# Two transfers for the transposition of x, largest scores ahead of rotated queries in two steps of four, and a high half behind the next exponents

## The reference

```python
x = x + xattn(layernorm(x), ctx, ctx, Wq, Wk, Wv, Wo)
x = x + ffn(layernorm(x), w_gate, w_up, w_down)

# xattn: q, k, v = h @ Wq, ctx @ Wk, ctx @ Wv, split in 16 heads; rotary embedding on q and k
score = einsum('bhqd,bhkd->bhqk', qh, kh) / sqrt(32)
out = einsum('bhqk,bhkd->bhqd', softmax(score), vh)      # then merged heads @ Wo

# ffn: act_qdq rounds to 16 bits by the tensor's largest magnitude; weights to 4 bits in blocks of 32
h = act_qdq(h)
up, gate = act_qdq(h @ qdq(w_up).T), act_qdq(h @ qdq(w_gate).T)
gate = act_qdq(gate * fixed_qdq_u16(sigmoid(gate)))
out = act_qdq(gate * up) @ qdq(w_down).T
```

## Time and profile before

| | us |
|---|---|
| median of 3 runs | 2328.13 (2327.36 to 2330.8) |
| the profiled execution | 2326.45 |
| its span, first to last instruction | 2324.6 |
| PE busy | 2203.7 (95%) |
| DVE busy | 1685.1 (72%) |
| ACT busy | 1329.8 (57%) |
| POOL busy | 701.5 (30%) |
| PE busy, 200 to 300 / 300 to 400 / 500 to 600 us | 87.3 / 93.1 / 93.7 |

### The profile page before, as it was taken

One profiled execution on the slowest core, in us unless ns is written; L12 is line 12 of the kernel. 1 busy time (PEld: TensorE's weight loads), 2 busy tenths in 40 slices (PEclk: granted clock), 3 DMA queues, 4 the chain that ended last, 5 costly groups with the idle time before them and its releaser, 6 DMA issues. The chain is left out here.

```text
span 2324.6 us, 31131 instructions
## 1 busy us (share of the span) xinstructions
PE 2203.7 (95%) x12037; PEld 971.1 (42%) x12037; DVE 1685.1 (72%) x1690; ACT 1329.8 (57%) x1299; POOL 701.5 (30%) x655
## 2 busy tenths in 40 slices
PE   5898999999998899999999999999998799999999
PEld 3443333333333444444444444444443344444444
DVE  7656788889876766445543598888888887778773
ACT  3345566666654233222322787877877777777772
POOL 3444566666664301000100264444444000000000
PEclk8899999999999999999999999999999899999999
DMA  6333667777777577888875898877776555655552
GB/s 189 97 103 101 168 173 189 170 193 173 193 169 182 154 232 244 265 245 254 255 229 180 286 336 306 303 283 290 292 281 260 188 223 221 235 220 204 209 217 91
DMA packets 286711, 500.14 MB, mean 215 GB/s; under 512 B 187500, under 2 KB 189804, under 8 KB 249692
## 3 DMA queue, kind: packets, MB, share of 16 engines
q1 hardware_dynamic: 286556, 498.09, 66.9%
HBM read 247.75 MB, written 186.58 MB: 187 GB/s over the span
## 5 line engine op out<-in xcount | busy, mean ns | idle before, releaser
L1694 PE MATMUL banks<-XB,W 128*128 128x512 f16 x2304 | 498.9, 380 | 2.3 <-ACT XB L1720 2.3
L1694 PE MATMUL banks<-XB,WT 128*128 128x512 f16 x2304 | 497.4, 379 | 0.0
L2160 PE MATMUL banks<-W,OH 128*128 128x512 f16 x2256 | 488.8, 380 | 2.5 <-DVE OH L2262 2.5
L1714 ACT ACTIVATE OB<-banks,uns 128x512 f32<-128x512 f32 x384 | 255.7, 684 | 391.2 <-PE banks L1694 388.6
L1694 PEld LDWEIGHTS banks<-XB,W 128*128 128x128 f16 x2304 | 225.7, 98 | 275.1 <-issue 3.4
L1694 PEld LDWEIGHTS banks<-XB,WT 128*128 128x128 f16 x2304 | 225.4, 98 | 271.8
L2160 PEld LDWEIGHTS banks<-W,OH 128*128 128x128 f16 x2256 | 221.1, 98 | 270.2 <-DVE OH L2262 3.0
L1981 POOL TENSOR_TENSOR PR<-GS,OB 128x2048 f32<-128x2048 f32 x46 | 220.6, 4795 | 257.5 <-ACT OB L1714 247.6
L1803 DVE TENSOR_REDUCE amx<-OB 128x1 f32<-128x2048 f32 x48 | 109.7, 2285 | 238.2 <-ACT OB L1714 238.2
L748 PE MATMUL banks<-XC,AH 128*128 128x512 f16 x768 | 179.3, 385 | 3.2 <-POOL AH L1506 1.6
L689 PE MATMUL banks<-XD,WQ 128*128 128x512 f16 x768 | 179.2, 383 | 2.5 <-DVE WQ L1127 1.2
(11 more groups left out here) (272 smaller groups left out, 2904.5 us busy)
## 6 DMA issues: line engine op xcount, KB each, us to landing
g_s<-OB SPq DMA_DIRECT2D x48, 1024.0 KB, 6.1
GL<-g_s SPq DMA_DIRECT2D x48, 1024.0 KB, 7.5
up_s<-OB SPq DMA_DIRECT2D x48, 1024.0 KB, 4.9
XA<-up_s SPq DMA_DIRECT2D x32, 1024.0 KB, 9.3
gq_s<-GQ SPq DMA_DIRECT2D x48, 512.0 KB, 4.8
XD<-gq_s SPq DMA_DIRECT2D x48, 512.0 KB, 6.7
XA<-in_x SPq DMA_DIRECT2D x16, 1024.0 KB, 6.7
QW<-QE SPq DMA_DIRECT2D x128, 128.0 KB, 2.9
```

The lines of the kernel that those rows point to most:

```text
L1694: t = e.matmul(pk[:].rearrange("p (j t) -> p j t", j=4), WT[w][:, ot, wa, kk, :], XB[i % 2][:, xa, :, kk, :], start=(kk == 0 and wa == 0 a ...
L1714: e.activation(OB[n % 3][:, r, :], bank[(k + 4) % 8][:], ACT.Copy, scale=uns[:, 12 * w + ot:12 * w + ot + 1]).then_inc(s_ev, 1)
L2160: t = e.matmul(pk[:].rearrange("p (r n) -> p r n", r=4), OH[i % 2][:, a, ot, j * 128:(j + 1) * 128], WD[:, :, c, wa, o4, :], start=(ot == ...
```

## The change

Three edits, all in the attention. `sp_x_turn` gets a half `a`, waits for the high parts (a = 0) or the low parts (a = 1) alone and transposes 16 blocks; up to step 15 both halves stand where the one transfer stood, later the first half stands in c = 1 at the old place and the second in c = 2, behind the swap and ahead of the load of x. All counts of `s_xt` double. `dve_largest` is the old maxima block as a function, and in steps 16 to 65 with c = 0 or c = 3 it is called ahead of the rotary addition. `act_a_high` is the old high half as a function; from step 16 on, the second unit's is called in the next step behind the exponents.

```diff
-            e.wait_ge(s_xlo, 2 * b + 2)
+            e.wait_ge((s_xhi, s_xlo)[a], 2 * b + 2)
...
-            e.dma_start_transpose(XD[b % 2][:].rearrange("p a j (k t) -> p (a j k) t", t=128),
-                                  ST.rearrange("p a j d -> p (a j d)")).then_inc(s_xt, 16)
+            e.dma_start_transpose(XD[b % 2][:, a, :, :].rearrange("p j (k t) -> p (j k) t", t=128),
+                                  ST[:, a, :, :].rearrange("p j d -> p (j d)")).then_inc(s_xt, 16)
...
                 for nb in [1] if s == 2 else x_at(s, 2):
-                    sp_x_turn(e, nb)
+                    sp_x_turn(e, nb, 0)
+                    if s < 16:
+                        sp_x_turn(e, nb, 1)
+                for nb in x_at(s - 1, 2) if s > 16 else []:
+                    sp_x_turn(e, nb, 1)
                 if c == 2 and 2 <= b + 2 < B:
                     sp_x_load(e, b + 2)
...
                     e.activation(P[0:SK], PB[0:SK, 0:4, :], ACT.Exp, scale=SM_SCALE).then_inc(s_p, 1)
+                for u in normal_at(s - 1)[1:] if s > 16 else []:
+                    act_a_high(e, u)
...
-                for u in normal_at(s):
...
+                for u in normal_at(s)[:1] if 16 <= s < NSTEP - 1 else normal_at(s):
+                    act_a_high(e, u)
...
+                largest_first = 16 <= s < NU + 2 and c in (0, 3)
+                if largest_first:
+                    dve_largest(e, s - 2)
                 if 1 <= s <= NU:
                     dve_rope_add(e, ROT["q", s - 1])
...
-                if 0 <= u < NU:
...
+                if 0 <= u < NU and not largest_first:
+                    dve_largest(e, u)
```

More of the change, by code:

```diff
@@ L424, in sp_x_load, with sp_x_turn @@
             e.dma_start(X[:], x1_rows(b)).then_inc(s_x, 16)
-        def sp_x_turn(e, b):
-            e.wait_ge(s_xlo, 2 * b + 2)
+        def sp_x_turn(e, b, a):
+            e.wait_ge((s_xhi, s_xlo)[a], 2 * b + 2)
             if b == 1:
@@ L561, in sp_attention @@
                         else:
-                            e.wait_ge(s_xt, 16 * (B - 1))
+                            e.wait_ge(s_xt, 32 * (B - 1))
                         e.wait_ge(s_x1d[0], 32 * (i + 1))
@@ L680, in pe_queries @@
             if c == 0 and b:
-                e.wait_ge(s_xt, 16 * b)
+                e.wait_ge(s_xt, 32 * b)
             for n, (a, xa) in enumerate(THREE):
@@ L939, in act_x_high @@
             if b >= 2:
-                e.wait_ge(s_xt, 16 * (b - 1))
+                e.wait_ge(s_xt, 32 * (b - 1))
             for h in range(2):
@@ L949, in act_largest, with act_a_high @@
             e.activation(MT[:], BQ_, ACT.Copy, scale=(QS * QS if 4 * b >= HALF else 1.0) / MS).then_inc(s_mte, 1)
+        def act_a_high(e, u):
+            nb, nc_ = divmod(u, 4)
+            e.wait_ge(s_an, u + 1)
+            if nb >= 2:
+                e.wait_ge(s_o, 4 * (nb - 2) + 4)
+            elif u == 0:
+                e.wait_ge(s_v, 16)
+                e.wait_ge(s_ct, 32)
+            e.activation(AH[nb % 2][:, 0, nc_, :], A[:, u % 6, :], ACT.Copy).then_inc(s_ah, 1)
         def act_attention(e):
@@ L1260, in dve_w_levels, with dve_largest @@
             e.tensor_tensor(v3(ld), v3(li), bc(scl), ALU.mult).then_inc(s_wx, 1)
+        def dve_largest(e, u):
+            mb, mc = divmod(u, 4)
+            e.wait_ge(s_sm, u + 1)
+            if u == 0:
+                e.wait_ge(s_const, NCONST)
+            if mc == 0 and mb >= 2:
+                e.wait_ge(s_mt, mb - 1)
+            e.tensor_reduce(MX[mb % 2][:, :, :, mc].rearrange("p j g -> p g j"),
+                            PB[:, 0:4, 0:4 * SK].rearrange("p g (j s) -> p g j s", j=4), AX.X, ALU.max).then_inc(s_mx, 1)
         def dve_attention(e):
```

## The result

The changed kernel takes 2339.74 us in the median of five runs (2338.97 to 2342.87), the kernel before 2328.13: a ratio of 1.0049, with a 95% interval of 1.0036 to 1.0062. It is slower, by 11.6 us, 2.3 us under the forecast. The profiled execution took 2339.03 us with a span of 2337.2, which is 12.6 us over the span before.

The account below looks back on a forecast made before the run. A ring of SP, DMA, DVE and POOL sets the period, not PE. Per group +2.07 - 0.6 - 0.6 = +0.85, ten groups +8.5, start +1.7, end +3.5: +13.7, so 2342 us on the median, range 2316 to 2354.

Parts of the forecast that it names:

- The ring: Closed loop of SP, DMA, DVE and POOL, transposition to transposition, 38.4 us; forecast +0.85 us per group, +8.5 over ten.
- Maxima first in c = 0: On DVE, MX ahead of the reciprocal in c=0 makes it 2.07 us later: +2.07 us per group.
- Statistics at the load: DVE ready sooner in c=3, but its statistics wait for the load, landing 17.2 us after the transposition began: -0.6 per group.
- No wait for the low parts: The first half of the transposition waits for the high parts of x only: -0.6 us per group.
- The start: Step 16: reciprocal 5.6 us later, some 1.3 hidden by the swap, 2.7 of low-part wait gone: +1.7 us.
- The end: Step 64: reciprocal falls behind MX, +4.7 us; the 1.17 us for P at 659.91 go: +3.5 us.
- DVE's wait for the load in nearly all groups: Sign that the forecast is right: DVE's statistics wait for the load of x, by 2 us and more.
- PE waits for P in c = 1: New PE wait of 1 to 2.5 us, from the later shift of x; costs nothing while the ring is longer.
- The early load: Rival: the load of x lands at about 15.1 us, ring 37.2 against 38.4, 2321 us; 14 in 100.
- The named waits: Rival: PE's 12.6 us for MX and 7.4 for P vanish, nothing replaces them: 2308 us; 6 in 100.
- The pieces: Rival: they cancel, the ring stays at 38.4 and only start and end are left: 2328 to 2333 us; 18 in 100.
- The dearer cut: Rival: cutting the transposition delays the load by 2 us in each group: 2362 us; 4 in 100.

Follow-up runs that it names:

- e2: The changed kernel without largest scores first in c = 0 (c = 3, split transposition and moved high halves stay): 2320.86 us, ratio 0.9966.
- e5: The kernel before with the largest scores first in c = 3 alone: 2325.72 us, ratio 0.9985.
- e1: The kernel before with the largest scores first in c = 0 alone: 2349.2 us, ratio 1.0094.
- e13: The changed kernel with the one unsplit transposition of before; largest scores first and moved high halves stay: 2339.86 us, ratio 1.0051.
- e7: The kernel before with the reciprocal at the start of its DVE step in c = 0, ahead of the residual sum: 2336.19 us, ratio 1.0031.
- e11: The changed kernel with both halves of the first split pair of the steady part (block 4) waiting for the low halves: 2340.98 us, ratio 1.0053.
- e3: The kernel before with the split transposition of x alone: 2318.27 us, ratio 0.9950.
- e4: The kernel before with the second high half moved behind the next exponents alone: 2334.08 us, ratio 1.0013.
- e12: The kernel before with the split transposition and largest scores first in c = 3, nothing else: 2318.19 us, ratio 0.9956.
- e6_load_first: The changed kernel with the load of x issued ahead of the low half's transposition: 2333.22 us, ratio 1.0010.
- e8_split_load: The kernel before with the split transposition and the load of x ahead of the low half, without the other edits: 2326.89 us, ratio 0.9982.

## Why the prediction was right, and where it was wrong

**The ring: right in size, by other terms.** +0.85 us a group was forecast and +0.85 measured (39.27 - 38.42), in the forecast as +2.07 - 0.6 - 0.6. The runs confirm the ring and the part that costs; that the sum comes out to the hundredth is luck, since its terms were off by -0.5, +0.7 and -0.2. The runs give +1.53 for the largest scores in c = 0 (e2 to after) and -0.68 for the rest (before to e2).
- *Maxima first in c = 0: mis-sized.* The reciprocal did start 8.06 us after the statistics, for a forecast of 8. What I missed stands one step on: the RB read waits for the landing of the write-out, and that took 1.50 us instead of 2.01, as x1 out, ahead of it on SP, now leaves 5.1 us before it instead of 3.1. So 0.42 us came back in "rec to RB" (2.70 to 2.28).
- *Statistics at the load: right alone, not in company.* e5 shows the gain in "X to st" (-0.81 for a forecast of -0.6), in the changed kernel it is +0.10. DVE does come with the load (slack 0.02 for 0.65), but the load lands 17.87 us after X instead of 17.14. I had let it land as before and put nothing for the cut; the halves hold SP for 5.47 and 2.75 us, where I had 3.4 each and 3.9 as the upper bound.
- *No wait for the low parts: right in size, credited to the wrong edit.* "RB to X" fell by 0.80, for 0.6, and SP's idle time ahead of the transposition from 0.70 to 0.10. But e1 and e13, which have no split, show the same (-0.92 and -0.68, idle 0.1).
- The two gains were added as if each had its own stretch. They share the one from the RB read to the statistics: 29.63 us before, 28.93 after, -0.70 instead of -1.2.

**The start: wrong in sign.** Forecast +1.7; the first transposition of the ten groups came at 259.38 instead of 264.43, -5.05. Part by part: -1.1 was there before any edit of the steady part (statistics at 204.44 for 205.53); kernels without the split have it too (203.64 in e7). The statistics of step 15 came another 3.2 us sooner, which the forecast had left out: the pair in step 13 was the first whose first half could leave without the low parts, at 222.51 instead of 230.29. I had looked for that gain only from step 16 on. By e11 it is worth 2.0 of the 3.2; the other 1.2 come in e1 too, which has no split, and stay open. Then the reciprocal, 3.9 us later for a forecast of 5.6:

```profile
238.66 2.46 DVE L1155 BATCH_NORM_STATS2 st<-XA 128x6 f32<-128x512 f32 x4
...
243.22 2.16 DVE L1280 TENSOR_REDUCE MX<-banks 128x16 f32<-128x1920 f32 x1 [1.69 <-PE banks L716]
...
245.90 0.55 DVE L1222 RECIPROCAL RG<-RG 128x64 f32<-128x64 f32 x1
```

And 4.6 us were absorbed behind it, for a forecast of 1.3 + 2.7: from this reciprocal to the transposition it is 18.1 us before (246.31 to 264.43) and 13.5 after, and 13.4 in e1 and e13, which have no split, so the order in c = 0 is enough for it. -1.1 - 3.2 + 3.9 - 4.6 = -5.0. Against the kernel before, this transposition is 0.8 and 2.1 us earlier in e13 and e1, and 4 to 9 us in all kernels with the split.

**The end: mis-sized.** Forecast +3.5; from the last transposition to the end it is 1685.1 us instead of 1676.0, +9.1. The kernel before has the shortest end of all fourteen profiles, so part of the 9.1 may be its own luck. The forecast priced step 64 and forgot step 60: its reciprocal also stands behind the maxima, and no transposition comes after it that could count it in a group. It starts 24.51 us after the last transposition instead of 19.94, +4.6. The maxima alone don't account for that: it is 23.7 to 24.3 us in e2, e3, e4 and e12 too, which have the old order there. From there to the reciprocal of step 64 it is 45.8 for 40.0, +5.8, for a forecast of 4.7, and from there on -1.2. The 5.8 can't be laid to the change alone: this stretch took 34.6 to 46.3 us among the twelve kernels of the experiments, 41.8 in e7_recip_first, whose code from step 64 on is that of before. PE's turn of the maxima there waits for queries whose swap lands late:

```profile
702.24 1.11 PE L726 MATMUL banks<-id,MX 128*128 128x128 f32 x4 [7.99 <-ACT QE L1011]
...
749.08 5.28 PE L752 MATMUL banks<-XC,AH 128*128 128x512 f16 x12 [4.62 <-POOL AH L1523]
```

Start and end were wrong by -6.8 and +5.6 and nearly cancelled. The time was hit closer than its parts.

Another mark spreads the same 12.6 us otherwise. Counted from reciprocal to reciprocal, it is 246.31 to 245.90 at the start (-0.4), 38.39 to 39.15 for each of eleven groups (+8.4), and 1656.0 to 1660.6 behind the last (+4.6). These can't be held against the forecast's +1.7, +8.5 and +3.5, which count from the transposition. At this mark its start is the 5.6 us by which the reciprocal was to come later, and it came 0.4 sooner: the start stays the worst miss.

**PE's waits.** The forecast of DVE's wait for the load in nearly all groups was right (32.1 us, ten times). That PE waits for P in c = 1, by 1 to 2.5 us, came true in nine of ten groups, by 1.61 to 1.94 us. The view lays six of these to the rotated queries (10.0 us) and three to P (5.1 us), but in all nine the largest scores start 0.25 to 0.28 us after the end of P. The addition that writes QR ends 0.12 to 0.14 us before them in six, but 5.7 us before in two, and in one (485.37) only after they have started, so it isn't what they wait for. Ten times PE waits for RX (13.6 us), behind the load, which I had not followed. The four parts add up to the group without any of these waits. The new P wait and RX wait in one group:

```profile
407.93 0.39 PE L716 MATMUL banks<-W,QE 32*128 32x120 f16 x16 [1.61 <-ACT P L986]
...
436.60 2.76 PE L752 MATMUL banks<-XC,AH 128*128 128x512 f16 x12 [1.08 <-DVE RX L1197]
```

**The rivals.** The early load is refuted for this change: the load landed 17.87 us after X, not 15.1. The named waits went and others took their place. The pieces didn't cancel: the ring went to 39.27. The dearer cut, 2 us a group, is refuted by e3_split_only, whose groups became shorter; what the cut costs is 0.5 us at the landing of the load (17.87 for 17.33 in e13). The Trainium skill ("DMA: Bandwidth & Descriptors", section "Anatomy of one DMA — SWDGE (gpsimd) path") has about 2.0 us of fixed cost for each DMA of another issuing path. SP's own time does not show it: 4.43 us for two halves back to back, 4.89 for the whole. The time from issue to landing may: at the least 4.4 us for 16 blocks in the changed kernel and 6.8 for 32 in the kernel before, so by an estimate from these two 2.0 us would be left for no blocks.

## What to carry to other kernels

When several engines close a ring through a DMA, cut the period at fixed events and compare the parts, before against after: a gain that one part shows may be given back in the next, and two gains in one stretch do not add. When a part shrinks, ask which edit did it, by a run without that edit: here the wait for the low parts went by the order on DVE and not only by the split made for it. Take as the mark an event that the edit doesn't move, and price the first and last pass of the loop with the same terms as the middle ones. An operation moved forward on an engine that isn't the busiest still costs a good part of its length if it passes the one operation that a transfer waits for, here 1.05 us (e1) to 1.53 (inside the change) of 2.07. And look at what a transfer stands behind: a small one on the critical path lands later when large ones leave right ahead of it.

## What the runs showed of the hardware

The time that a transposition holds SP depends on what is in flight more than on its size. The low half, 16 blocks, held SP 1.8 to 3.6 us behind the swap in the changed kernel and 5.2 to 7.9 us right behind the 1 MB load in e6_load_first. The whole of 32 blocks held it 5.2 to 7.9 us in the kernel before and 7.0 to 9.5 in e13_without_split, where the same transfer met another mix. So issuing a transfer sooner lengthened the issue of the next one, and the queue behind both waited.

The landing of a small transfer went by what left ahead of it. The write-out of the reciprocals (128 x 64 f32) landed 1.5 us after its issue when x1 out had left 5.1 us before it (changed kernel), 2.0 us with 3.1 us between them (kernel before), 2.6 with 2.3 (e8_split_load) and 3.8 with 0.9 (e7_recip_first). It isn't the distance alone: e2_without_c0 has 1.4 us with 3.4 between them. Which of the transfers in flight holds it up, no run separates.
